# A recurrent stage whose PSUM sums are kept and added to, in place of being rebuilt at each step

## The reference

```python
def step(h, x_t):
    combined = jnp.concatenate([broadcast(h), enc_hiddens], axis=2)      # enc_hiddens: 77 rows of context
    score = jnp.einsum('bsh,h->bs', jnp.tanh(combined @ W_att), V_att)
    attn = jax.nn.softmax(score, axis=-1)
    context = jnp.einsum('bs,bsh->bh', attn, enc_hiddens)
    gz, gr, gh = jnp.split(jnp.concatenate([x_t, context]) @ Wi + b, 3)
    rz, rr, rh = jnp.split(h @ Uh, 3)
    z, r = sigmoid(gz + rz), sigmoid(gr + rr)
    hh = jnp.tanh(gh + r * rh)
    h_new = z * h + (1.0 - z) * hh
```

## Time and profile before

| | us |
|---|---|
| median of 3 runs | 4579.9 (4578.97 to 4592.61) |
| span of the profiled execution | 4575.7 |
| the recurrence's loop within it | about 252 to 2284 |
| all that comes before | about 252 |
| all that comes after | about 2292 |

### The profile page before, as it was taken

How to read it: one execution, slowest core, us unless ns; L and a number is a source line. 1 busy time by engine, 2 the same in 40 slices (tenths; PEclk the granted TensorE clock), 3 DMA queues, 4 the chain that set the end, 5 groups by cost and what they waited for, 6 DMA issues and landing times. The chain is left out here.

```text
span 4575.7 us, 82192 instructions
## 1 busy us (share of the span) xinstructions
PE 4041.4 (88%) x25247; PEld 2348.8 (51%) x25308; DVE 2805.4 (61%) x13508; ACT 2308.3 (50%) x6560; POOL 948.4 (21%) x4509
## 2 busy tenths in 40 slices
PE   7889999999999999999899999778888888888868
PEld 2367777777777777777733334322333333333222
DVE  3466666666666666666654454546666666666534
ACT  5355565555555555555533334214555555555423
POOL 0323333333333333333331000300000000100002
PEclk9999999999999999999999999758888888888879
DMA  0100000000000000000001000011111111111100
GB/s 9 56 2 2 2 2 2 2 2 2 2 2 2 2 2 2 2 2 2 6 31 37 1 1 1 22 57 45 45 57 45 57 57 45 57 52 49 33 30 5
DMA packets 48838, 94.48 MB, mean 21 GB/s; under 512 B 11296, under 2 KB 31792, under 8 KB 48144
## 3 DMA queue, kind: packets, MB, share of 16 engines
q1 hardware_dynamic: 48400, 89.22, 6.0%
HBM read 72.88 MB, written 15.39 MB: 19 GB/s over the span
## 5 line engine op out<-in xcount | busy, mean ns | idle before, releaser
L939 PE MATMUL ps<-g_h,w_p 128*128 128x128 f32 x4096 | 918.2, 306 | 0.0
L2280 ACT ACTIVATE t_ex<-ps 128x1024 f32<-128x1024 f32 (+1 forms) x480 | 471.8, 1021 | 571.8 <-PE ps L2227 558.1
L939 PEld LDWEIGHTS ps<-g_h,w_p 128*128 128x128 f32 x4096 | 616.7, 190 | 0.0
L935 PE MATMUL ps<-g_h,w_p 128*128 128x77 f32 x2048 | 456.5, 304 | 174.5 <-DVE g_h L1009 145.9
L2375 DVE TENSOR_REDUCE t_ncol<-ps 128x1 f32<-128x512 f32 x768 | 486.6, 685 | 154.6 <-PE ps L2200 154.0
L1005 DVE SCALAR_TENSOR_TENSOR g_used<-g_encg,g_e 128x77 f32<-128x77 f32 x3072 | 550.3, 230 | 0.0
L975 ACT ACTIVATE g_th<-ps 128x77 f32<-128x77 f32 x1024 | 241.4, 236 | 535.5 <-PE ps L935 535.5
L1051 POOL TENSOR_SCALAR g_z<-g_tzr 128x1 f32<-128x1 f32 x1024 | 194.7, 190 | 1363.0 <-ACT g_tzr L984 1363.0
L935 PEld LDWEIGHTS ps<-g_h,w_p 128*128 128x128 f32 x2048 | 304.5, 188 | 310.3 <-DVE g_h L1009 295.5
L956 PE MATMUL ps<-g_th,g_vrep 128*128 128x77 f32 x2048 | 456.6, 305 | 0.0
L1014 DVE TENSOR_REDUCE g_ntop<-ps 128x1 f32<-128x77 f32 x1024 | 244.1, 238 | 338.2 <-PE ps L956 337.3
(11 more groups left out here) (481 smaller groups left out, 6910.3 us busy)
## 6 DMA issues: line engine op xcount, KB each, us to landing
t_qst<-t_turn_q SPq DMA_DIRECT2D x288, 96.0 KB
t_kst<-t_turn_k SPq DMA_DIRECT2D x144, 96.0 KB
t_turn_q<-t_part SPq DMA_DIRECT2D x24, 384.0 KB, 2.5
t_turn_k<-t_part SPq DMA_DIRECT2D x12, 384.0 KB, 3.3
t_wf<-in_t_wf SPq DMA_DIRECT2D x6, 514.5 KB, 5.5
m_experts<-in_experts SPq DMA_DIRECT2D x1, 3072.0 KB, 12.7
t_wa<-in_t_wa SPq DMA_DIRECT2D x6, 448.0 KB, 3.4
t_wx<-in_t_wx SPq DMA_DIRECT2D x6, 448.0 KB, 4.2
```

The lines of the kernel that those rows point to most:

```text
L935: M(att[c], w["att_h"], h[t % 2][:, c:c + 1].broadcast_to([P, S]), start=False, stop=True, skip_group_check=True).then_inc(*st.sem("att", c))
L939: return M(G[c][:, g], weights, h[t % 2][:, c:c + 1].broadcast_to([P, P]), start=False, stop=last, skip_group_check=True)
L2280: A(ex[0:kw, slot[pf, c, l, n]], ps[0:kw, at:at + 2], ACT.Exp, scale=SCALE).then_inc(*st.sem(f"{pf}e{n}", c))
```

## The change

The bf16 splits are gone (`encs`, `gxs`, `split_slice`), and with them the three-part matmuls of each step. PSUM now keeps the sums: `att` and the gates' sums stay open, and each step adds the product with the *increment* of the state, `dh`, to them. The gates' bank holds 128 positions' columns for each gate; every 128 steps (`t % SPAN == 0`) `fill` lays down `gx` for the next 128 positions by three fp32 matmuls with the identity, `plain` gets a zero, `att` is laid down anew from `encp`, and the product is taken with the whole state once. In between each product with `Uh` adds to all 128 columns, and step `t` reads column `t % 128`. The candidate's product has 129 columns, the last of which is the sum without `gx`.

The state is kept in `hist` (all 513 of them). VectorE's `update` computes `dh = (hh - h)(1 - z)`, so that GpSimd computes only 1-z (`factor`, one instruction) and, behind it, `hist` (`advance`, one instruction). `x_res` is added to once at the end, by two VectorE instructions over 512 positions, in place of GpSimd's addition in each step.

The order changes in two places. TensorE takes the products of both gates ahead of `scores`. VectorE computes `g_zr` ahead of the third weighted sum hm.

```diff
-        gx = sb("gx", [P, B, T, 3])
+        gx = sb("gx", [P, B, 3, T])
...
-                nc.scalar.activation(gx[:, 1, :, g], ps[:, 6 + g % 2], ACT.Identity, bias=w["bi"][:, g:g + 1])\
+                nc.scalar.activation(gx[:, 1, g], ps[:, 6 + g % 2], ACT.Identity, bias=w["bi"][:, g:g + 1])\
...
+                def moved(c, t, n):
+
+                    a = hist[:, c, t:t + 1] if t % SPAN == 0 else dh[t % 2][:, c:c + 1]
+                    return a.broadcast_to([P, n])
...
                 def attend(c, t):
-                    if t:
-                        pe.wait_ge(*st.at("h", c, t - 1))
-                    M(att[c], w["att_h"], h[t % 2][:, c:c + 1].broadcast_to([P, S]), start=False, stop=True,
+                    if t % SPAN == 0:
+                        if t:
+                            pe.wait_ge(*st.at("h", c, t - 1))
+                        M(att[c], k.ident[:], encp[:, c], start=True, stop=False, skip_group_check=True)
+                    else:
+                        pe.wait_ge(*st.at("dh", c, t - 1))
+                    M(att[c], w["att_h"], moved(c, t, S), start=False, stop=True, skip_group_check=True).then_inc(*st.sem("att", c))
+
+                def fill(c, t):
+                    for g in range(3):
+                        M(gates[c][:, g], k.ident[:], gx[:, c, g, t:t + SPAN], start=(g == 0), stop=False, skip_group_check=True)
+                    M(plain[c], k.ident[:], zero[:], start=False, stop=False, skip_group_check=True)
+
+                def recur(c, t, g):
+                    return M(gates[c][:, g], w["uh"][:, g * D:(g + 1) * D], moved(c, t, SPAN), start=False, stop=False,
...
+                def recur_candidate(c, t):
+                    M(ps[:, 4 * c + 2, 2 * SPAN:3 * SPAN + 1], uhh[:], moved(c, t, SPAN + 1), start=False, stop=True,
...
                 for t in range(T):
                     for c in range(B):
                         attend(c, t)
-                        open_gates(c, t)
+                        if t % SPAN == 0:
+                            fill(c, t)
+                        recur(c, t, 1)
+                        recur(c, t, 0)
                         scores(c, t)
-                        close_gates(c, t)
-                        if t + 1 < T:
-                            open_att(c)
+                        recur_candidate(c, t)
...
                     weigh("r", 1, c)
                     weigh("z", 0, c)
-                    weigh("hm", 2, c)
                     dve.wait_ge(*st.at("gates", c, t))
                     dve.wait_ge(*st.at("z", c, t))
-                    fma("zr", c, zr[:, c], mac[:, c, 0:2], sinv[:, c:c + 1], G[c][:, 0:2, 0])
+                    fma("zr", c, zr[:, c], mac[:, c, 0:2], sinv[:, c:c + 1], gates[c][:, 0:2, t % SPAN])
+                    weigh("hm", 2, c)
                     dve.wait_ge(*st.at("hm", c, t))
...
                 def update(c, t):
-                    if t >= 2:
-                        dve.wait_ge(*st.at("saved", c, t - 2))
-                    dve.wait_ge(*st.at("zh", c, t))
+                    if t:
+                        dve.wait_ge(*st.at("h", c, t - 1))
+                    dve.wait_ge(*st.at("omz", c, t))
                     dve.wait_ge(*st.at("cand", c, t))
-                    fma("h", c, h[1 - t % 2][:, c:c + 1], hh[:, c:c + 1], omz[:, c:c + 1], zh[:, c:c + 1])
+                    V.scalar_tensor_tensor(out=dh[1 - t % 2][:, c:c + 1], in0=hh[:, c:c + 1], scalar=hist[:, c, t:t + 1],
+                                           in1=omz[:, c:c + 1], op0=ALU.subtract, op1=ALU.mult).then_inc(*st.sem("dh", c))
...
+                for c in range(B):
+                    dve.wait_ge(*st.at("h", c, T - 1))
+                    V.tensor_tensor(k.x[:, c], k.x[:, c], hist[:, c, 1:T + 1], ALU.add).then_inc(summed, 1)
...
+                def advance(c, t):
+                    pool.wait_ge(*st.at("dh", c, t))
+                    nc.gpsimd.tensor_tensor(hist[:, c, t + 1:t + 2], hist[:, c, t:t + 1], dh[1 - t % 2][:, c:c + 1], ALU.add)\
```

More of the change, by code:

```diff
@@ L818, in gru_stage @@
         identb = sb("identb", [P, P], BF16)
[L819 to L820 removed]
+        zero = sb("zero", [P, 1])
         uhh = sb("uhh", [P, D])
         vrep = sb("vrep", [P, P])
[L823 removed]
+        hist = sb("hist", [P, B, T + 1])
+        dh = [sb(f"dh{i}", [P, B]) for i in range(2)]
         th, e = sb("th", [P, B, S]), sb("e", [P, B, S])
@@ L900, in _ @@
                     dve.wait_ge(*pre.at(f"g{g}", 0))
[L901 to L909, removed]
-                dve.wait_ge(*ev.at("gx2"))
[L911 to L919, removed]
+                    V.tensor_scalar(gx[:, 0, g], ps[:, 2 + g % 2], w["bi"][:, g:g + 1], None, ALU.add).then_inc(*ev.sem(f"gx{g}"))
+                dve.wait_ge(*ev.at("gx2"))
+        SPAN = P
+        att = [ps[:, 4 * c, 0:S] for c in range(B)]
+        score = [ps[:, 4 * c + 1, 0:S] for c in range(B)]
+        gates = [ps[:, 4 * c + 2, 0:3 * SPAN].rearrange("p (g n) -> p g n", n=SPAN) for c in range(B)]
+        plain = [ps[:, 4 * c + 2, 3 * SPAN:3 * SPAN + 1] for c in range(B)]
         st = Steps(k, "g", 2, pe="att score gates", act="tanh exp tzr cand",
-                   dve="top sinv r z hm zr in h", pool="z1 omz zh saved")
+                   dve="top sinv r z zr hm in dh", pool="omz h")
+        summed = k.semaphore("g_summed")
         with nc.Block() as block:
@@ L938, in recur @@
-                def recur(c, t, g, weights, last=False):
-                    return M(G[c][:, g], weights, h[t % 2][:, c:c + 1].broadcast_to([P, P]), start=False, stop=last,
-                             skip_group_check=True)
-                def open_gates(c, t):
-                    if t and t % SLICE == 0 and c == 0:
-                        pe.wait_ge(sliced, SPLIT * (t // SLICE + 1))
-                    for i in range(3):
-                        M(G[c][:, :, 0], identb[:], gxs[:, i, c, t:t + 1].rearrange("p o g -> p (o g)"),
-                          start=(i == 0), stop=False, skip_group_check=True)
-                    recur(c, t, 1, w["uh"][:, D:2 * D])
@@ L986, in candidate @@
                     act.wait_ge(*st.at("tzr", c, t))
-                    A(hh[:, c:c + 1], G[c][:, 2, 1:2], ACT.Tanh, bias=hin[:, c:c + 1], scale=tzr[:, c, 1:2])\
+                    A(hh[:, c:c + 1], plain[c], ACT.Tanh, bias=hin[:, c:c + 1], scale=tzr[:, c, 1:2])\
                         .then_inc(*st.sem("cand", c))
```

59 lines of the change are left out of this document (15 added, 44 removed).

## The result

The changed kernel took 4616.05 us (median of 4 runs, 4603.63 to 4626.82), the kernel before 4584.6 beside it: 1.007 times as long, interval 1.0049 to 1.009. The change made the kernel slower by 0.7%, where about no change was forecast and 4613 was the upper end of the range. The kernel before itself came out at 4584.6 in these runs, 4.7 above the 4579.9 from which the forecast started.

The account below looks back on a forecast made before the run. The latency of one chain's step (3.94 us) was taken to bound the kernel, not any engine's queue. Terms 0 + 5 - 0.2 + 1.5 - 1 = +5.3 took the median from 4579.9 to 4585 us, range 4562 to 4613.

Parts of the forecast that it names:

- The sum of VectorE's and GpSimd's parts: Chain's step: later hh loses 0.09 us, update no longer waiting for three GpSimd instructions gains 0.09; together 0.00.
- the bound of 20: Rounding error allowed on the step's latency: -0.02 to +0.02 us per step, or -10 to +10 us over 512 steps.
- TensorE's part: nothing: Matmuls of each step: removing six of eleven and moving a product ahead of the scores changes 0 per step.
- this rival's case: TensorE's clock falls to 1.2 GHz as its busy share drops: 4.4 us a step, about 4820 us; 3 in 100.
- Laying down: Sums laid down anew every 128 steps: about 1.4 us each of three times, 1.0 at the start, together +5.
- Final additions, prologue, casts: Two additions at the end +1.5 us, ten VectorE instructions gone ahead of the loop -0.2, GpSimd's casts gone -1.
- The cheap update wait: At the update: `dh` starts 0.04 behind hh, so the step loses 0.09 us, 4539 us; 8 in 100.
- own waits: VectorE's wait for its own result is free: zr starts at 436.90, -0.14 us a step, 4513 us; 3 in 100.
- The condition by which two chains meet under 3.82: ScalarE's queue: a later hh holds up the other chain's exp once step latency is under 3.82; 4611 us, 7 in 100.

Follow-up runs that it names:

- e4: The kernel before with zr put ahead of hm as the only edit; 4602.7 us, ratio 1.004.
- e2: The changed kernel with three idle bf16 products of 77 columns per chain and step added behind the candidate's product; 4609.6 us, ratio 1.0066.
- e3: The changed kernel with the z gate's product moved behind the scores again; 4613.1 us, ratio 1.0077.
- e7: The kernel before without the three bf16 products that carry the encoder's part into the scores; 4584.0 us, ratio 1.0004.
- e11: e2 with SPAN = 64, so sums and products have 64 columns and are laid down every 64 steps; 5099.9 us, ratio 1.1138.
- e13: e2 with sums laid down every 64 steps, but products and laying-down kept at 128 columns (the last one 64); 4621.9 us, ratio 1.0113.
- e5: The changed kernel with the update itself carrying the wait for hh, and its wait for `h` left out; 4558.9 us, ratio 0.9946.
- e9: The changed kernel with hm ahead of zr, late waits carried by update, hh and zr themselves, and three idle products a step; 4439.5 us, ratio 0.9698.
- e10: The kernel before with only the order of waits turned: zr on z's sum, hh on tzr, update on z*h first; 4526.9 us, ratio 0.9889.

## Why the prediction was wrong

- **The sum of VectorE's and GpSimd's parts, 0.00 per step, was mis-sized.** The mechanism came out as written: zr no sooner, hin 0.41 behind zr (forecast 0.40), hh 0.04 behind hin, the update released by ScalarE. But the loss was 110 ns, not 90: zr starts 0.115 behind the read, not 0.10, and hin 0.41 later. The gain was 76 ns, not 90: the update starts 0.14 behind hh's end, not 0.13. The two differences of 90 were made from rows rounded to 0.01, three or four added in each; 34 ns was left, over the bound of 20 that I gave, and 512 times 34 is 17.4 us. A median over all steps would have told 0.115 from 0.10 in the trace of before, where zr waits for z's sum too. That 0.13 came so near for the update was in part luck: in the earlier trace rows GpSimd's product ended at 412.44, 0.03 behind hh, and the row names it as the releaser, so the 0.14 read there was not hh's price alone. What e4 adds: GpSimd's z*h doesn't wait for hin, so in the kernel before, too, the later hh costs only 37 ns (3984 to 3947).
- **"TensorE's part: nothing" failed in its clock.** The product ahead of the scores is free in an undisturbed step, as said. What I had put at 3 in 100, as a whole loop at half clock, came as ten stretches and cost 11.0 us; e2 gives it back, e3 has one stretch left with only z's product moved back behind the scores, and e7 makes such stretches in the kernel before. The row that I weighed was the mean of a long stretch, and the argument was that no gap passes half a microsecond. That was wrong for the changed kernel: there TensorE's idle time ahead of each `attend` is 0.46 for one chain and 0.55 for the other in the median (0.57 in the row at 435.69), where before it was 0.12 and 0.22, and VectorE's pauses make it 0.92. e11 shows that this rival's case, half clock for the whole loop, exists, at 5100 where I had 4820: halving the width of the products brings it about.
- The Trainium skill, "TensorE: Matmul & The Clock Gate", part 1, ties the slower clock to idle gaps of TensorE. The trace of the changed kernel agrees in that each stretch follows a pause. But gaps of 0.92 at 816.0 and 0.93 at 1331.4 were followed by no fall, and in e11 the clock fell behind gaps of 0.74 at most and stayed down with TensorE marked busy throughout. Idle gaps alone don't tell it.
- **Laying down**: +5 forecast for three times and the start; 6.2 for three. The scores' delay was as said (0.84 for "about 0.85"), but both chains are held in turn, 2.1 in place of 1.4 each time, and the 1.0 at the start was not seen (the first update at 255.9, before at 256.0). e13 confirms 2.2 each.
- **Final additions, prologue, casts**: +1.46 and -0.1 measured for +1.5 and -0.2. The casts' -1 was not to be seen: other stalls came to 9.8 in place of 8.6.
- **Rivals.** The cheap update wait was wrong for this program, but e5 shows that it hangs on how its waits are written. For own waits, the same: the Trainium skill, "VectorE: DVE Perf Modes", section "The DRAIN you can't avoid", says a semaphore between chained instructions costs nothing extra, measured there on eight copies. It says too that a next instruction that isn't held starts sooner, so hm's 0.16 behind z doesn't speak against it, as the prediction had it. Here zr's wait for z's sum costs 122 ns in an instruction of its own and 43 on zr. The condition by which two chains meet under 3.82 was worked out for hh at 3.46 behind its update, and it moves with hh. In e9 hh stands at 3.28, so that the same sum gives 3.45, and its free steps of 3.66 don't test it. In e5 hh stands at 3.49 and the sum gives 3.87 to 3.88, just what its step has (3876), and nothing was lost yet. What happens below the limit stays open.

In sum: 17.4 in place of 0, 11.0 in place of 0, 6.2 in place of 5 and 1.3 in place of -1 make the 35.9 of the loop. The first two are the steps that failed. The median passed the upper end of the range by 3 us only, and the kernel before had moved by 4.7 between the two sets of runs; but 28 us of growth that the sum had at nothing are no matter of spread.

## What to carry to other kernels

When the chain's latency sets the pace, write the wait that comes last so that it rides on the instruction, and leave fulfilled ones to the waiting instruction ahead: here three such turns, one wait left out and one reordering took the changed kernel from 4616 to 4437 us. Don't pull an instruction ahead of one that was filling a wait. When work is taken off TensorE, look at the clock stretch by stretch, not at its mean, and keep products wide; and make a sum of small differences from medians over the loop, never from one rounded timeline.

## What the hardware showed that I had not expected

- The same wait costs 34 to 43 ns on the instruction and 89 to 141 in a separate waiting instruction: VectorE on itself 43 and 122, on ScalarE 34 and 141, on GpSimd 34 and 89 (e10, before), ScalarE on itself (hh behind tzr's end) 34 and 94. The update's waiting instruction (the 141 and the 89) holds two semaphores, the others one. A late wait for TensorE wasn't tried.
- Products of 64 columns in place of 128, with all else alike, put the clock at 1.2 GHz for a whole loop of 2540 us, while TensorE was marked busy 99.7%. What exactly the chip takes as work wasn't settled.
- VectorE pauses of 0.25 to 0.37 us come again every 64 steps, at places in the program that move with the edits. Their cause wasn't tried. Each of the ten falls of the clock in the changed kernel came behind one, but most pauses were followed by none. In e5 two of the three falls came at a laying-down instead, behind a gap of 0.73 on TensorE in which it waited for GpSimd's `hist`.
